# Mixture-of-experts block: the following block's rows, split and gates in every block, and the low parts of the weights moved

## What is computed

```python
logits = x @ Wr + br                      # 8192 tokens, 8 experts
top_vals, top_idx = jax.lax.top_k(logits, 2); w = softmax(top_vals)
cap = ceil(8192 / 8 * 1.25)               # 1280 places for each expert
kv, ki = jax.lax.top_k(key_mat, cap)      # an expert's 1280 heaviest tokens
xe = x[tok]
h1 = gelu(einsum('ech,ehf->ecf', xe, W1) + b1, approximate=False)
y = einsum('ecf,efh->ech', h1, W2) + b2
out = zeros_like(x).at[tok].add(y * gate)
return _layer_norm(out + hidden_states, gamma, beta)
```

## Time and profile before

| what | us |
|---|---|
| median of 3 runs (lowest to highest) | 1322.94 (1322.87 to 1324.41) |
| profiled execution | 1321.82 |
| its span | 1320.1 |
| busy of the span: PE, DVE, ACT, POOL | 1150.9, 979.1, 747.8, 932.4 |
| mean granted TensorE clock | 0.93 of full |

### The profile page before, as it was taken

One profiled execution on the slowest core, in us unless ns is written; L12 is line 12 of the kernel. 1 busy time (PEld: TensorE's weight loads), 2 busy tenths in 40 slices (PEclk: granted clock), 3 DMA queues, 4 the chain that ended last, 5 costly groups with the idle time before them and its releaser, 6 DMA issues. The chain is left out here.

```text
span 1320.1 us, 23670 instructions
## 1 busy us (share of the span) xinstructions
PE 1150.9 (87%) x5959; PEld 764.9 (58%) x5960; DVE 979.1 (74%) x2249; ACT 747.8 (57%) x1454; POOL 932.4 (71%) x1075
## 2 busy tenths in 40 slices
PE   6899999999999999999999999999987128989800
PEld 4556566666666565656666665656644115989800
DVE  5888687777777676777777777767776787777676
ACT  5565667565666656575655666566642440444436
POOL 5576968787877969797878778796965202545438
PEclk9999999999999999999999999999998556999955
DMA  4000101010101101010201011010101511424296
GB/s 155 18 19 17 49 18 65 2 65 1 64 18 46 49 16 48 16 65 0 64 1 64 16 48 33 18 34 17 47 3 53 139 64 21 108 33 112 28 307 206
DMA packets 68494, 70.91 MB, mean 54 GB/s; under 512 B 12928, under 2 KB 64048, under 8 KB 68288
## 3 DMA queue, kind: packets, MB, share of 16 engines
q1 hardware_dynamic: 46816, 47.18, 11.2%
q10 hardware_dynamic: 16896, 16.78, 3.8%
q0 software_dynamic: 4704, 6.11, 3.0%
HBM read 40.35 MB, written 29.45 MB: 53 GB/s over the span
## 5 line engine op out<-in xcount | busy, mean ns | idle before, releaser
L721 ACT ACTIVATE PF<-PS 128x512 f32<-128x512 f32 x512 | 298.3, 595 | 259.5 <-PE PS L1140 251.4
L1022 DVE TENSOR_REDUCE NMAX<-PS 128x1 f32<-128x512 f32 x512 | 342.6, 681 | 91.4 <-PE PS L1149 87.7
L583 POOL TENSOR_TENSOR SF<-SF,PF 128x512 f32<-128x512 f32 x252 | 322.4, 1301 | 15.7 <-ACT PF L721 15.5
L1221 PE MATMUL PS<-PF,V 128*64 128x512 f32 x1024 | 249.4, 608 | 0.0
L1139 PE MATMUL PS<-Q,K 128*128 128x512 f32 x512 | 222.0, 434 | 2.3 <-ACT PF L721 2.2
L1149 PE MATMUL PS<-K,Q 128*128 128x512 f32 x512 | 206.2, 403 | 11.2 <-DVE NMAX L1022 11.0
L1140 PE MATMUL PS<-Q,K 128*128 128x512 f32 x512 | 201.9, 394 | 0.0
L740 ACT ACTIVATE Q<-PS 64x512 fp32r<-64x512 f32 x256 | 151.5, 592 | 45.2 <-PE PS L172 40.3
L660 POOL TENSOR_TENSOR XL<-XF,XH 128x512 fp32r<-128x512 f32 x63 | 82.8, 1314 | 131.5 <-ACT XH L798 131.5
L1139 PEld LDWEIGHTS PS<-Q,K 128*128 128x128 f32 x512 | 96.4, 188 | 120.3 <-issue 56.4
L580 POOL TENSOR_TENSOR SF<-PF 128x512 f32<-128x512 f32 x126 | 161.9, 1300 | 5.2 <-ACT PF L721 4.7
(11 more groups left out here) (364 smaller groups left out, 2415.0 us busy)
## 6 DMA issues: line engine op xcount, KB each, us to landing
X<-in_L_attn_x SPq DMA_DIRECT2D x16, 512.0 KB, 3.5
MODB<-mod_rows SPq DMA_DIRECT2D x16, 512.0 KB, 3.7
h_rows<-H ACTq DMA_DIRECT2D x16, 512.0 KB, 3.0
acc_rows<-H ACTq DMA_DIRECT2D x16, 512.0 KB, 4.1
out_x<-X SPq DMA_DIRECT2D x16, 512.0 KB, 2.9
A<-acc_rows SPq DMA_DIRECT2D x15, 512.0 KB, 8.9
W1F<-in_L_ffn_W SPq DMA_DIRECT2D x3, 1024.0 KB
W2F<-in_L_ffn_W SPq DMA_DIRECT2D x3, 1024.0 KB, 7.3
```

Source lines behind the costliest of these rows:

```text
L583: s_sum.done(pool.tensor_tensor(total, total, tile, ALU.add))
L721: s_exp.done(act.activation(PF[:, u % 8, :], st_bank(u), ACT.Exp))
L1022: s_mred.done(dve.tensor_reduce(NMAX[:, p % 2, r:r + 1], mx_bank(u), AX.X, ALU.max, negate=True))
L1221: last = pe.matmul(num_bank(p)[odd * R:(odd + 1) * R, :], V1[:, vp, c, :], PF[:, k % 8, :], start=(c == 0), stop=(c == TC - 1))
```

## The change

What DVE and PE did at an expert's start for its first block (transposes, split, gates) is done in the block ahead of it, as for all others, also across experts, and once for a dummy block behind the last. The transposes stand behind step 6 (`TURN`), not 4. The second half of W1L and W2L are made in front of DVE's loop for the first expert, and behind YS of an expert's last block for the next. PE's loop loads no expert number, its first load stands ahead of the busy matmuls, which move to `experts` and use W1H. POOL gathers once more behind the loop. SP waits for W2L and the split before it reads back.

```diff
-        pe.wait_ge(s_iot, 2)
-        for k in range(BUSY):
-            pe.matmul(kt_ps, ZP[:, :], NUMB[:, 0:T // RING, :].rearrange("p a r -> p (a r)"), start=True, stop=True)
...
+    GATES_USED, BUSY, TURN = 6, 16, 6
...
+    def expert_of(eng, a):
+        return eng.value_load(INFO[0:1, bass.ds(a, 1)], min_val=0, max_val=E - 1)
+    def each(eng, first, middle, last, number=None, named=True):
+        with eng.Fori(0, actives(eng) if number is None else number) as a:
+            e = expert_of(eng, a) if named else None
...
         for late in range(2):
             g = total + late
+            if late == 0:
+                s_t.wait(pool, g, -1)
+                s_gate.wait(pool, g, -1)
             s_tok.wait(pool, g, -1)
             s_tok.done(gate(5))
             s_tok.wait(pool, g, 0)
+            if late == 0:
+                gate(2)
+                gather()
             shift(g)
...
-        def expert(e, a, g):
-            next_gates(e, g)
-            split_tokens(g)
-            low_weights_1(dve, m, a, 1)
+        def low_weights_2(a):
             s_w2h.wait(dve, a, 0)
             s_w2l.done(dve.tensor_tensor(W2L[:, :, :], W2F[:, :, :], W2H[:, :, :].bitcast(F32), ALU.subtract))
         def block(e, a, g, more):
+            following = e if more else expert_of(dve, a + 1)
...
-                if f == 5 and more:
-                    next_gates(e, g + 1)
-            if more:
-                split_tokens(g + 1)
-            else:
+                if f == 5:
+                    next_gates(following, g + 1)
+            if not more:
                 low_weights_1(dve, m, a + 1, 0)
+            split_tokens(g + 1)
...
+        def last(e, a, g, k):
+            block(e, a, g, False)
+            low_weights_1(dve, m, a + 1, 1)
+            low_weights_2(a + 1)
         dve.wait_ge(s_b, 32)
-        each(dve, expert, lambda e, a, g, k: block(e, a, g, True), lambda e, a, g, k: block(e, a, g, False))
+        low_weights_1(dve, m, 0, 1)
+        low_weights_2(0)
+        next_gates(expert_of(dve, 0), 0)
+        split_tokens(0)
+        each(dve, None, lambda e, a, g, k: block(e, a, g, True), last)
...
         def expert(e, a, g):
-            transposes(g)
             s_w1l.wait(pe, a, 0)
...
-                if f == 4 and more:
+                if f == TURN:
                     transposes(g + 1)
...
+        number = actives(pe)
+        s_w1h.wait(pe, 0, 1)
+        for k in range(BUSY):
+            pe.matmul(PS[:, 4, :], W1H[:, 0, 0:P], W1H[:, 0, 0:F // 2], start=True, stop=True)
         pe.wait_ge(s_b1, 1)
+        transposes(0)
+        each(pe, expert, lambda e, a, g, k: block(e, a, g, True), lambda e, a, g, k: block(e, a, g, False), number, False)
...
-        m["xs"]["w2h"].wait(sp, nact, 0)
+        m["xs"]["w2l"].wait(sp, nact, 0)
+        m["xs"]["xl"].wait(sp, total, KC - 1)
```

More of the change, by code:

```diff
@@ L1260, in route @@
     FAR = 4.0 * NT
-    BUSY = 16
     EQ, n1 = sb("EQ", [P, NCH, E]), TC * (NB - EARLY)
@@ L1665, in experts @@
     MAXB, LEAD = CAP // BLK, 3
-    GATES_USED = 6
+    GATES_USED, BUSY, TURN = 6, 16, 6
     assert CAP % BLK == 0
@@ L1698, in actives @@
         return eng.value_load(INFO[0:1, 3 * E:3 * E + 1], min_val=1, max_val=E)
-    def each(eng, first, middle, last):
-        with eng.Fori(0, actives(eng)) as a:
-            e = eng.value_load(INFO[0:1, bass.ds(a, 1)], min_val=0, max_val=E - 1)
+    def expert_of(eng, a):
[3 more added lines that the diff above has]
+            e = expert_of(eng, a) if named else None
             more = eng.value_load(INFO[0:1, bass.ds(a + E, 1)], min_val=1, max_val=MAXB - 1)
@@ L1743, in shift, with gather @@
             s_tok.wait(pool, g, 3)
+        def gather():
+            for t in range(BT):
+                off = bass.IndirectOffsetOnAxis(ap=TOKN[:, t:t + 1], axis=0)
+                pool.indirect_dma_start(out=XG[:, t, :], out_offset=None, in_=m["h2_dram"], in_offset=off).then_inc(s_gx.sem, 16)
         def block(e, a, g, k):
@@ L1754, in block @@
             gate(1)
-            for t in range(BT):
-                off = bass.IndirectOffsetOnAxis(ap=TOKN[:, t:t + 1], axis=0)
-                pool.indirect_dma_start(out=XG[:, t, :], out_offset=None, in_=m["h2_dram"], in_offset=off).then_inc(s_gx.sem, 16)
+            gather()
             shift(g)
@@ L1910, in _ @@
         pe.transpose(xt_bank[:, 0:E * FC], B1R[:, :], IDENT[0:E * FC, 0:E * FC]).then_inc(s_b1t, 1)
+        number = actives(pe)
+        s_w1h.wait(pe, 0, 1)
+        for k in range(BUSY):
+            pe.matmul(PS[:, 4, :], W1H[:, 0, 0:P], W1H[:, 0, 0:F // 2], start=True, stop=True)
         pe.wait_ge(s_b1, 1)
-        each(pe, expert, lambda e, a, g, k: block(e, a, g, True), lambda e, a, g, k: block(e, a, g, False))
+        transposes(0)
+        each(pe, expert, lambda e, a, g, k: block(e, a, g, True), lambda e, a, g, k: block(e, a, g, False), number, False)
 def last_norm(nc, out, m, sem, sb, block):
```

## The result

Twenty runs of the changed kernel have a median of **1325.62 us** (1323.83 to 1327.30), twenty of the kernel before beside them 1322.66 (1321.81 to 1324.70). Forecast were 1323.6 and a range of 1318.2 to 1326.2. The profiled execution took 1324.64 (span 1322.9), against 1321.82 (1320.1) before.

A forecast was written before the change was run, and what follows sets the result against it. TensorE is packed inside an expert, so only the start, the change of expert and the end count: +0.25 - 2.05 + 2.5 = +0.7 on 1322.94 gives 1323.6 us; range 1318.2 to 1326.2.

The forecast's parts named there:

- DVE's loads are not hidden: Rival at the change of expert: DVE's register loads begin only after W2L; +2.9 in all, 1325.8 us, chance 0.1.
- Start, +0.25: First block: POOL's index copy and gate wait for DVE, so transposes come 0.45 later; +0.25 us in the end.
- POOL is not held: Rival: POOL's small instructions do not wait for DVE; start gives 3.4, end costs only 1.6; 1317.5 to 1319, chance 0.18.
- Change of expert, -3.55 and +1.5 for the clock: Change of expert: W2 products come 3.55 us earlier, but PE's 2.3 idle makes the clock fall, costing 1.5; -2.05 together.
- The 0.94 for the rows: Change of expert: PE's wait of 0.94 us for the following block's rows goes, as part of the -3.55.
- Steady blocks, 0: Blocks inside an expert: later transposes and split, and an extra expert load on DVE, change nothing; 0 us.
- The owed transposes (0.35): Change of expert: four transposes move into the block ahead, adding 0.35 us on PE there and taking it off later.
- YS behind the split, +1.6: Last block: YS now waits on DVE for the first half of W1L and the split; +1.6 us.
- Gate beside the second half of W1L, +0.9: End: POOL's gate ahead of the last scatter waits until DVE finishes the second half of W1L; +0.9 us.
- The gather instructions themselves I cost at nothing more: Start, on POOL: gather instructions take no longer beside DVE's work, about their usual 1.0 us beside W1L; 0 added.
- The end's bound of +3: End: the last norm was forecast to move by +2.5 us, with bounds +1.4 and +3.

The follow-up runs named there:

- Experiment 1: Changed kernel with the first expert's second half of W1L and W2L moved behind the split of block 0; 1325.81 us, ratio 1.0023 to the kernel before.
- experiment 5: Experiment 1 with SP's load of the next expert's weights one block later; 1320.87 us, ratio 0.9992 to the kernel before.
- Experiment 3: Changed kernel with W2L made by eight DVE instructions instead of one; 1322.21 us, ratio 0.9989 to the kernel before.
- experiment 2: Changed kernel with YS ahead of the split in an expert's last block; 1321.20 us, ratio 0.9981 to the kernel before.
- experiment 4: Changed kernel with W2L made by two DVE instructions, one eighth and the other seven; 1324.36 us in one run.
- experiment 6: Changed kernel with only SP's load of the next expert's weights one block later; 1324.68 us, ratio 1.0014 to the kernel before.
- experiment 7: Changed kernel with the edits of experiments 1, 2 and 5 together; 1317.63 us, ratio 0.9965 to the kernel before.
- experiment 8: Experiment 7 with eight unread matmuls between an expert's third and fourth product; 1317.17 us, ratio 0.9958 to the kernel before.

## Why the prediction was right in its range and wrong in one term

The kernel came out 2.0 above the forecast and 0.6 below the upper end of the range. That end was set for the rival "DVE's loads are not hidden" (1325.8), which did not happen: HH stands right behind W2L. That the missing term below fits into the range is luck.

- **Start, +0.25: right.** The first W2 product came 0.66 later, 0.26 with the 0.4 taken off; the transposes at 1117.5 by the same count, against 1117.7. POOL was held as worked out from the earlier trace rows: the copy 0.90, the gate 2.13. PE took its loads ahead of the warming matmuls, and DVE's lay in its idle time. What the prediction did not see is that the rival "POOL is not held", priced at 3.4 for the start, had a floor: the scatter's landing, which was just hidden before (about 1134.2, with YS at 1134.32). Experiment 1 shows the gain gone, experiment 5 shows it back.
- **Change of expert, -3.55 and +1.5 for the clock: right.** The first W2 product was forecast at 1188.6, the start's 0.25 not counted, and came at 1189.03, or 1188.6 with the 0.4 off. The 0.94 for the rows is gone, the loads hid under W2L, PE waited 2.01 (forecast 2.3), the clock then fell, for 3.4. Experiment 3 gives its price as 1.5.
- **Steady blocks, 0: right.** From the second pair of W2 products to the last YS it took 55.5 before and 58.3 now (from 1191.10). The owed transposes (0.35), the rest of the low clock (1.0) and YS's 1.6 make up 58.5.
- **YS behind the split, +1.6: right.** With a start and a change of expert of -1.8 together, YS should stand 0.2 earlier; it stands 0.07 earlier, 0.47 with the offset.
- **Gate beside the second half of W1L, +0.9: right**: 1.10 instead of 0.19.
- **"The gather instructions themselves I cost at nothing more": wrong, and this is the step that failed.** The last scatter's issue was treated the same way: the end stopped at the gate, and W2L, which starts right behind that W1L, was looked at only for SP's new wait. The issue of the scatter, 1.56 before, took 3.44 beside W2L: **+1.9**. The step's reason, that beside W1L one took about its usual 1.0, names no row. The two issues that fit it, in the kernel before at the change of expert, were no test: one began at 1186.42, ahead of W1L's 1186.76, the other at 1187.75, 0.14 before that W1L handed over, and took 1.07. The start of that same kernel had a test (DVE, then POOL):

```profile
1119.64 1.22 DVE L1636 TENSOR_TENSOR W1L<-W1F,W1H 128x1024 fp32r<-128x1024 f32 x1
1120.77 2.29 DVE L1825 TENSOR_TENSOR W2L<-W2F,W2H 128x2048 fp32r<-128x2048 f32 x1
```

```profile
1120.47 1.23 POOL L1757 DMA_INDIRECT XG<-h_rows,TOKN  x1 [0.30 <-issue]
1121.72 1.38 POOL L1738 TENSOR_TENSOR TOKS<-TOKP,NOUGHT 128x2 uint32<-128x2 uint32 x1
```

This gather's issue began 0.30 before W1L handed over and took 1.23, the longest of the 20 there (0.96 to 1.13 otherwise); the copy behind it is a second case of 1.38 beside W2L, where the prediction speaks of one.

With 1.9 the sum is 0.7 + 1.9 = +2.6, against +3.0 measured by median and +2.8 in the profiled executions. The end's bound of +3 was short too; it came to 1.6 + 0.9 + 1.9 = 4.4, and experiment 2 got 4.0 of it back; PE's four transposes, 0.35, stay.

The Trainium skill ("SBUF — State Buffer", Who interferes with whom) holds a GpSimd instruction that reads SBUF back for the length of a DVE instruction with two SBUF inputs; for the copy and the gates the trace agrees (0.90, 2.13, 1.10 against 0.19). The same section takes a `tensor_tensor` not to hold a DMA that GpSimd issues, and infers as the reason that writing the descriptors needs the write side of the shared ports, of which a `tensor_tensor` takes only the read side; here the measurement decides, 3.44 against 1.57 and 2.66 against 1.06. An indirect DMA also has its row numbers in SBUF (TOKN, TOKS). Whether it is their reading that waits, no run here tells.

Open: what makes the clock fall or not. Behind a wait of 2.0 to 2.1 at the change of expert it fell in the changed kernel and in experiments 4, 5 and 6, and it held in experiment 1 behind 2.00 and in experiment 3 behind 2.49. Behind an idle of 1.92 ahead of the first product it fell in experiments 2 and 7, and held in 8. The idle time alone doesn't tell them apart. How often it falls in each kernel was not settled, and of experiment 3's surplus over its expectation only the one profiled execution speaks.

## What to carry to other kernels

When long DVE instructions with both operands in SBUF are moved, list every POOL instruction due beside the new place, and the issues of indirect DMAs with them: each is held until the running one ends, and one after another each can meet the next. Put such DVE work behind the last short POOL step that something waits for, or cut it into pieces. Before counting a gain at a start, look for what lands next: a buffer that a transfer still holds limits it as much as an engine does, and a bulk load that starts beside that transfer moves the limit.

## What the runs showed of the hardware that was not expected

- The issue of an indirect DMA on POOL waits out a DVE instruction with two SBUF operands that began before it: scatter 3.44 against 1.57, gather 2.66 against 1.06. One that began 0.05 ahead of such an instruction took 1.63. With pieces of about 0.35 instead of 2.28 the scatter at the end took 1.58.
- The landing of an indirect scatter took 7.5 beside a 2 MB load on another queue, and 3.8 without it.
- DVE's register loads cost nothing beside a DVE instruction of 2.28 (HH stands right behind W2L). At the start of the changed kernel, with nothing there to cover them, DVE idles 3.17 before HH, 1.33 of it after ACT had HF ready (1122.20).
- The same idle of PE (2.0) was followed by a clock of 0.50 of full for about 3.4 in some kernels and by none in others.
